# Preparing stage of a graph and attention layer: centred weights, x also loaded by features, the row norm applied where products are read

## What is computed

```python
xn = _layernorm(x, axis=-1)
h = xn @ W                                       # graph branch
deg = segment_sum(edge_weight, dst) + 1.0
dinv = rsqrt(deg)
norm = dinv[src] * edge_weight * dinv[dst]
agg = segment_sum(norm[:, None] * h[src], dst) + (dinv * dinv)[:, None] * h
k = elu(xn @ Wk.T) + 1.0                         # attention branch, 8 heads
v = xn @ Wv.T
context = einsum('bhnd,bhne->bhde', k, v)
```

## Time and profile before

| | us |
|---|---|
| median of 3 runs | 1871.64 (1870.88 to 1873.41) |
| the profiled execution, whole time | 1867.27 |
| its span in the trace | 1865.2 |
| PE busy | 1507.2 (81%) |
| POOL busy | 1020.2 (55%) |
| DVE busy | 980.8 (53%) |
| ACT busy | 521.9 (28%) |

### The profile page before, as it was taken

The page is one execution under the profiler, slowest core; times in us unless marked ns, Lnnn a source line. Parts: engine busy times, 40 slices in busy tenths (PEclk is TensorE's granted clock), DMA queues, the critical chain, the costliest instruction groups (busy, mean ns, idle before and its releaser), DMA issues. The chain is left out here.

```text
span 1865.2 us, 34354 instructions
## 1 busy us (share of the span) xinstructions
PE 1507.2 (81%) x7942; PEld 1216.4 (65%) x7943; DVE 980.8 (53%) x3382; ACT 521.9 (28%) x1456; POOL 1020.2 (55%) x1069
## 2 busy tenths in 40 slices
PE   5499986887697888698688778866479999999987
PEld 4366645665575666476576656645269989988976
DVE  8766546554446555365365517536843333343457
ACT  0144432121121121121112112101035555555533
POOL 0200016777777777777777777772035544544545
PEclk9699996999797999798799987977589999999999
DMA  6000033333333333333333333333922232354266
GB/s 224 1 0 0 0 129 98 107 105 104 101 104 104 104 104 105 101 105 105 104 103 104 104 102 104 104 105 105 178 70 96 69 118 74 93 161 144 71 206 248
DMA packets 102895, 194.20 MB, mean 104 GB/s; under 512 B 24032, under 2 KB 59360, under 8 KB 102720
## 3 DMA queue, kind: packets, MB, share of 16 engines
q0 software_dynamic: 48336, 132.17, 24.5%
q1 hardware_dynamic: 54512, 61.52, 10.9%
HBM read 160.02 MB, written 33.60 MB: 104 GB/s over the span
## 5 line engine op out<-in xcount | busy, mean ns | idle before, releaser
L707 POOL DMA_INDIRECT ring<-table,staged x784 | 747.5, 953 | 242.8 <-issue 226.9
L982 PE MATMUL bank<-ring,hots 128*128 x1372 | 324.6, 391 | 54.4 <-SPq L696 54.4
L982 PEld LDWEIGHTS bank<-ring,hots 128*128 128x128 f32 x1372 | 264.4, 195 | 104.7 <-issue 68.5
L1379 POOL DMA_INDIRECT got_x<-rows,at_x x114 | 110.2, 967 | 206.3 <-DVE at_x L1497 183.7
L982 PE MATMUL bank<-ring,late_hots 128*128 x388 | 139.9, 511 | 97.8 <-SPq L696 90.8
L1474 PEld LDWEIGHTS bank<-xT,w 128*128 128x128 f32 x1696 | 208.7, 194 | 15.5 <-issue 10.2
L1474 PE MATMUL bank<-xT,w 128*128 128x128 f32 x1696 | 209.8, 278 | 8.6 <-issue 8.6
L1447 ACT ACTIVATE hT<-bank,b 128x128 f32<-128x128 f32 x424 | 155.9, 368 | 182.7 <-PE bank L1474 158.6
L1482 PE MATMUL bank<-w,hT 128*128 128x256 f32 x848 | 201.0, 380 | 2.4 <-DVE y L1539 2.4
L792 DVE TENSOR_SCALAR hots<-iota_t,edge_l 128x128 f32<-128x128 f32 x686 | 182.4, 364 | 1.8
L982 PEld LDWEIGHTS bank<-ring,late_hots 128*128 128x128 f32 x388 | 90.9, 249 | 140.0 <-issue 126.1
(11 more groups left out here) (274 smaller groups left out, 2263.7 us busy)
## 6 DMA issues: line engine op xcount, KB each, us to landing
w<-in_w SPq DMA_DIRECT2D x32, 512.0 KB, 4.9
ring<-table,staged POOLq DMA_INDIRECT x784
got<-spread SPq DMA_DIRECT2D x11, 1024.0 KB, 8.7
x<-in_x SPq DMA_DIRECT2D x1, 6272.0 KB, 22.7
table<-xn SPq DMA_DIRECT2D x7, 896.0 KB, 4.4
rows<-xn SPq DMA_DIRECT2D x1, 6272.0 KB, 27.7
out<-out_c SPq DMA_DIRECT2D x12, 512.0 KB, 3.5
b<-in_b SPq DMA_DIRECT2D x16, 128.0 KB, 5.4
```

The costliest lines, as they stand in the source:

```text
L707: pool.indirect_dma_start(out=ring[:, j, :], out_offset=None, in_=a.table, in_offset=bass.IndirectOffsetOnAxis(ap=staged[:, half, col:col ...
L982: last = nc.tensor.matmul(agg, hot[:, k, :], two[:, k, :], start=False, stop=False)
L1379: pool.indirect_dma_start(out=got[:, n, :], out_offset=None, in_=a.rows, in_offset=bass.IndirectOffsetOnAxis(ap=at[:, n:n + 1], axis=0)).t ...
```

## The change

- **x by features.** The host also lays x out transposed (`x_cols`), and SP loads four tiles of it at a time into two slots (`xt`, 512 KB a DMA, 13 DMAs). PE multiplies it directly: no transposes and no copies of them.
- **Centred weights.** PE sums the columns of the key, graph and value weights with a matrix of ones (L474), and DVE subtracts the mean from each column (L326). A product of raw x with centred weights is the product of x minus its mean. The context sums use x times the row's rstd without its mean; the centred value weights take the mean out.
- **Norm where products are read.** ACT reads nk, pk (relu(k), new) and h with the row's rstd (or its negative) as scale. `cur` is x times rstd.
- **kk on POOL.** The sum of ek and pk is a POOL instruction (L452); DVE's L264 is gone. Four slots of `cur`, `kk` and the product bank in place of two, and the context of tile t-2 follows the keys of tile t.
- **Statistics first.** x is loaded in seven pieces, the first of seven tiles ahead of the weights. DVE starts with the statistics of these seven tiles, centres the weights, and makes batch 0; the other statistics stand between batches 1 to 5. The roots come in three parts.
- **Roots seeded on ScalarE.** ACT takes Ln and Exp as a seed, DVE refines it with one Newton step (`root`, L305). POOL's two powers are gone.
- **The tail.** The scaling of h (49 DVE instructions, L369) comes in one piece after the last root. SP issues the last piece of x_cols (tile 48) behind the first two writes of the table.
- `Combine` uses four semaphores for its loads in place of one for each; order and sizes of its DMAs stay.

```diff
-            sp.dma_start(m.x1[:], a.x.rearrange("(t p) d -> p t d", p=P)).then_inc(ld_x, 16)
-            sp.dma_start(m.weights[:], a.weights).then_inc(ld_w, 16)
-            sp.dma_start(next_i[:], a.next_cols).then_inc(ld_next, 16)
+            def columns(c):
+                if c >= 2:
+                    sp.wait_ge(kg_ok, (c - 1) * 4)
+                n = min(4, NT - c * 4)
+                sp.dma_start(xt[:, c % 2, 0:n], a.x_cols[:, c * 4:c * 4 + n]).then_inc(ld_xt[c % 2], 16)
+
+            for k, (t0, t1) in enumerate(XS):
+                sp.dma_start(m.x1[:, t0:t1], x[:, t0:t1]).then_inc(ld_x[k], 16)
+                if k == 0:
+                    sp.dma_start(m.weights[:], a.weights).then_inc(ld_w, 16)
+                if k < 2:
+                    columns(k)
+            sp.wait_ge(hot_ok, 1)
+            sp.dma_start(next_i, a.next_cols).then_inc(ld_next, 16)
...
+            for c in range(2, NT // 4):
+                columns(c)
+            stored(0)
+            stored(1)
+            columns(NT // 4)
+            for g in range(2, NT // 7):
+                stored(g)
```

DVE (`one_hots` is unchanged; `spreads` is one bn_stats a tile, `variance` the six small instructions after them):

```diff
+            def root(out, v, r, n):
+                c.add(dve.tensor_tensor(nt[:, 0:n], r, r, ALU.mult))
+                c.wait()
+                c.add(dve.scalar_tensor_tensor(nt[:, 0:n], nt[:, 0:n], -0.5, v, ALU.mult, ALU.mult))
+                c.wait()
+                c.add(dve.scalar_tensor_tensor(out, nt[:, 0:n], 1.5, r, ALU.add, ALU.mult))
+                c.wait()
...
+            spreads(0)
+            variance(0)
+            dve.wait_ge(csum_ok, 1)
+            for k, (w0, n) in enumerate(CENTRED):
+                for ch in range(DC):
+                    last = dve.scalar_tensor_tensor(m.weights[:, ch, w0:w0 + n], csum_ps[k], -1.0 / D, m.weights[:, ch, w0:w0 + n],
+                                                    ALU.mult, ALU.add)
+            last.then_inc(centred, 1)
+            one_hots(0, 0)
+            normal(0)
+            spreads(1)
+            spreads(2)
+            variance(1)
+            one_hots(1, 1)
+            normal(1)
+            one_hots(2, 0)
+            spreads(3)
+            one_hots(3, 1)
+            spreads(4)
+            one_hots(4, 0)
+            spreads(5)
+            spreads(6)
+            variance(2)
+            one_hots(5, 1)
+            normal(2)
+            with dve.Fori(0, (BATCHES - 6) // 2) as i:
                 for slot in range(2):
-                    one_hots(i * 2 + slot, slot)
...
+                    one_hots(i * 2 + (slot + 6), slot)
...
+            dve.wait_ge(seed_ok, 4)
+            root(m.dinv[:], var[:], seed[:], NT)
```

ACT, POOL and PE:

```diff
+            def keys(t, j):
+                kg, scale = kg_ps[j % 4], rstd[:, bass.ds(t, 1)]
+                if not isinstance(t, int) or t >= 4:
+                    act.wait_ge(ctx_mm, t - 2)
+                    settle(act, m)
+                act.activation(cur[:, j % 4, 0:D], tile(m.x1, t), ACT.Copy, scale=scale).then_inc(cur_ok, 1)
...
+                act.wait_ge(kg_ok, t + 1)
                 settle(act, m)
-                act.activation(nk[:], kg[:, 0:D], ACT.Relu, scale=-1.0).then_inc(nk_ok, 1)
-                act.activation(tile(hw, t), kg[:, D:2 * D], ACT.Copy).then_inc(hw_ok, 1)
+                act.activation(nk[:], kg[:, 0:D], ACT.Relu, scale=neg[:, bass.ds(t, 1)]).then_inc(nk_ok, 1)
+                act.activation(pk[:, j % 2], kg[:, 0:D], ACT.Relu, scale=scale)
+                act.activation(tile(hw, t), kg[:, D:2 * D], ACT.Copy, scale=scale).then_inc(hw_ok, 1)
                 act.wait_ge(nk_ok, t + 1)
...
+                if t == 3:
+                    seeds(1, var_ok, 2, *PARTS[1])
+                if t == 11:
+                    seeds(2, var_ok, 3, *PARTS[2])
...
+                if t == EVEN + 6:
+                    seeds(3, deg_ok, 1, 0, NT)
...
+            def keys(t, j):
+                pool.wait_ge(ek_ok, t + 1)
+                if not isinstance(t, int) or t >= 4:
+                    pool.wait_ge(ctx_mm, t - 2)
+                    settle(pool, m)
+                pool.tensor_tensor(kk[:, j % 4], ek[:, j % 2], pk[:, j % 2], ALU.add).then_inc(kk_ok, 1)
...
+            pe.wait_ge(centred, 1)
+            AFTER = {2: 1, 6: 2, 8: 3, 11: 4, 14: 5}
+            degrees(0, 0)
+            for t in range(16):
+                keys(t, t % 8, None if t % 4 else t // 8 * 16 + 16)
+                if t in AFTER:
+                    degrees(AFTER[t], AFTER[t] % 2)
+            with pe.Fori(0, 3) as i:
+                for j in range(8):
+                    keys(i * 8 + (j + 16), j, None if j % 4 else i * 16 + 48)
+                    if j % 4 != 3:
+                        n = j - j // 4
+                        degrees(i * 6 + (n + 6), n % 2)
```

More of the change, by code:

```diff
@@ L257, in one_hots @@
                 last.then_inc(hot_ok, 1)
[L259 to L268, removed]
@@ L289, in _ @@
-            dve.wait_ge(rstd_ok, 1)
-            dve.scalar_tensor_tensor(shift[:], mean[:], -1.0, rstd[:], ALU.mult, ALU.mult).then_inc(norm_ok, 1)
-            one_hots(FIRST_BATCHES + 1, 1)
-            dve.wait_ge(ld_next, 16)
-            c.add(dve.tensor_tensor(unsorted[:], dst_i[:], next_i[:], ALU.is_gt))
-            c.wait()
-            c.add(dve.reduce_sum(drops[:], unsorted[:], axis=AX.X))
[L298 to L303, removed]
@@ L336, in _ @@
             c.add(dve.tensor_scalar(m.half, m.half, 0.5, None, ALU.mult))
+            for t in range(35, NT):
+                scaled(t)
             c.wait()
@@ L355, in keys, with seeds @@
-            def keys(t, j, left=NT):
-                slot = j % 2
-                kg = kg_ps[slot]
+            act.preload_act_table_set("natural_log_exp_and_others")
+            act.sem_inc(hw_ok, 4)
+            def seeds(n, sem_in, count, t0, t1):
+                act.wait_ge(sem_in, count)
+                act.activation(ln_s[:, t0:t1], var[:, t0:t1], ACT.Ln).then_inc(ln_ok, 1)
+                act.wait_ge(ln_ok, n + 1)
+                act.activation(seed[:, t0:t1], ln_s[:, t0:t1], ACT.Exp, scale=-0.5).then_inc(seed_ok, 1)
@@ L375, in _ @@
[L375 to L386 removed]
+                settle(act, m)
+                act.activation(ek[:, j % 2], nk[:], ACT.Exp, scale=-1.0).then_inc(ek_ok, 1)
@@ L400, in _ @@
+            keys(LAST, LAST)
         @block.tensor
@@ L409, in _ @@
             pe.wait_ge(ld_const, 16)
+            pe.wait_ge(ld_w, 16)
+            for k, (w0, n) in enumerate(CENTRED):
+                for ch in range(DC):
+                    last = nc.tensor.matmul(csum_ps[k], m.ones, m.weights[:, ch, w0:w0 + n], start=(ch == 0), stop=(ch == DC - 1))
+            last.then_inc(csum_ok, 1)
             def degrees(b, slot):
@@ L450, in _ @@
-            turned(0, 0)
-            def both(i, t):
-                for half in range(2):
-                    degrees(i * 2 + FIRST_BATCHES + half, half)
-                    keys(t + 2 * half, 2 * half)
-                    keys(t + 2 * half + 1, 2 * half + 1)
-            both(0, 0)
-            with pe.Fori(1, TURNS) as i:
-                both(i, i * 4)
-            nc.tensor.matmul(deg_ps, zero[:, 0:P], zero[:, 0:3 * NT], start=False, stop=True).then_inc(deg_mm, 1)
-            for t in range(NT - LATE, NT):
-                keys(t, t % 4)
-                if t == NT - LATE + 1:
+                if not isinstance(t, int) or t >= 2:
+                    context(t - 2, (j - 2) % 8)
@@ L466, in _ @@
+            for t in range(EVEN, NT):
+                keys(t, t % 8, None if t % 4 else t // 8 * 16 + 16)
+                if t < EVEN + 4:
+                    degrees(t - EVEN + 24, (t - EVEN) % 2)
+                if t == EVEN + 3:
+                    nc.tensor.matmul(deg_ps, zero[:, 0:P], zero[:, 0:3 * NT], start=False, stop=True).then_inc(deg_mm, 1)
+                if t == EVEN + 7:
                     pe.wait_ge(deg_ok, 1)
```

218 lines of the change are left out of this document (104 added, 114 removed).

## The result

| | before | changed |
|---|---|---|
| median, four runs each | 1871.26 (1869.6 to 1873.41) | 1820.88 (1812.0 to 1823.18) |
| the profiled execution, whole time | 1867.27 | 1820.67 |
| its span | 1865.2 | 1818.8 |
| first gather of the next stage | 284.28 | 232.52 |

The changed kernel is faster: a ratio of 0.9721 (0.9687 to 0.9755). Forecast were 1821, with a range of 1812 to 1834, and a first gather near 234.

A forecast was written before the change was run, and what follows sets the result against it. Before: entry bound by DVE, then POOL; steady part by PE. Last table landing moves from 281.0 to 230.6, 50.4 less: 1867.27 becomes 1816.9, plus 4.4 for the median: 1821, range 1812 to 1834.

The forecast's parts named there:

- Entry: Start of the stage: weights land at 12.2, column sums 5.25, centring 2.5, one-hots 4.50, degrees 3.5; first keys at 28.0.
- Low clock after idling: PE in the entry runs slow after waits: column sums 5.25 (2.6 at best), degree batches 0 and 1 3.5 each.
- Batch 1: Second degree batch in the entry: PE has three tiles done at 34.2, waits 3.6 for DVE, ends the batch at 41.3.
- Seed of part 1: ACT's seed stands behind keys(3); DVE can begin batch 2 at 47.0, an added wait that holds its list for 9.
- Rate: Loop from tile 15: PE is the bound, a tile 2.63; four tiles with three batches take PE 16.3, DVE 14.9.
- DVE against POOL: POOL's kk additions beside DVE's one-hots: each costs DVE between 0 and 0.73, taken as 0.36.
- rival B: One-hots on DVE: each POOL addition costs 0.73, DVE becomes the bound; +4 to +11, 1825 to 1832; chance 0.25.
- Tail: End of the stage: scaling at 207.7, first write 209.6, DMA bounds the writes, 19.3 for 6.42 MB, last landing 230.6.
- Rival C: Table writes at the end go at the pace of another 49-tile write, 27.7 against 21.0: +6.7, 1828; chance 0.1.
- Rival D: The entry is cheaper, column sums and two batches on PE at full clock: 1813 to 1815; chance 0.15.
- Rival E: Tiles 0 to 48: PE falls to 1.2 GHz, slower than before, up to 150 more, up to 1970; chance 0.03.

The follow-up runs named there:

- number 11: The changed kernel again, without an edit, on the same chip as number 10: median 1816.18, ratio 0.9714 to the kernel before, first gather at 234.84.
- number 10: Changed kernel with the edits of number 6, number 7, Number 8, number 9, and PE's running sums two tiles earlier: median 1803.79, ratio 0.9644 to the kernel before.
- number 9: Changed kernel with 12 products of zeros on PE ahead of the column sums and 10 behind: 1812.46 in one execution, first gather at 231.56.
- Number 8: Changed kernel with degree batch 1 behind tile 4 in place of tile 2 on PE: first gather at 225.75, against 232.52.
- Number 5: Changed kernel with the seed of part 1 behind keys(0) in place of keys(3) in ACT's list: first gather at 232.70, against 232.52.
- number 1: Changed kernel with two transposes a tile put back on PE, results unused: first gather at 240.49, against 232.52.
- numbers 2: Changed kernel with every kk addition on POOL done twice, the second into an unread buffer: first gather at 240.76, against 232.52.
- number 3: Changed kernel with the 49 kk additions moved from POOL to DVE: first gather at 234.46, against 232.52.
- number 6: Changed kernel with the seed of the degrees ahead of keys(44) in place of keys(46) in ACT's list: first gather at 228.16, against 232.52.
- number 7: Changed kernel with the x_cols piece of tile 48 issued ahead of the table's writes: first gather at 232.43, against 232.52.

## Why the prediction was right, step by step

The first gather was forecast 50.4 earlier and came 51.8 earlier. The forecast of 1821 is met to 0.1, by more luck than the steps deserve: the profiled span fell by only 1865.2 - 1818.8 = 46.4. From first gather to end it is 1580.9 before and 1586.3 after, but 1581.2 in number 11, 1586.0 in number 10 and 1579.0 in number 9. The stages that nobody touched scatter by several us between executions, in part in the landing of rows: 27.7 before, and 30.4, 24.4, 25.5 and 26.2 in these four. So one whole execution tests my sum only to some 7 us, and the first gather tests it better. Two more terms cancelled: for the profiled execution the sum said 1816.9 and 1820.67 was measured, but I had added 4.4 for the median, which lay that far above the profiled execution before, and after the change it lay only 0.2 above.

- **Entry.** Weights 12.2, measured 13.19; sums 5.25, measured 5.03; centring 2.5, measured 1.95; first keys 28.0, measured 28.05. The errors cancelled: DMA a microsecond late, PE and DVE each a little faster.
- **Low clock after idling.** Right for batch 0 (3.5, measured 3.46) and batch 1 (3.5, measured 3.23). Missed: the keys behind batch 1 still took 2.40, and tile 48's 3.78, where the sum had them at full clock. The sums' 5.03 fits the low clock too, but the profile grants 1.00 from 13.2 to 18.0, so what made them slow is not shown. Number 8 shows the price of the early waits: 5.5, not the 3.4 that they last.
- **Batch 1.** PE waited 2.16 for DVE and 0.91 for POOL, forecast 3.6 for DVE alone. The term of 0.73 for a POOL addition left out its start: it stood behind hot_lo, 3.80 for two.
- **Seed of part 1.** A wait of 9 forecast, 7.58 measured, batch 2 at 46.31 (47.0). The sum said that PE would have four tiles done and wait 0.4, measured 0.30. Number 5 confirms that the wait is covered to within half a us.
- **Rate.** Four tiles and three batches 16.3; measured (177.90 - 112.93) / 4 = 16.24. PE is the bound: what number 1 gave it to do arrived at the end, and DVE's wait that number 5 removed did not.
- **DVE against POOL, rival B.** The bounds were 0 and 0.73, I took 0.36, and numbers 2 and 3 show means of 0.27 for the first addition and 0.37 for a second. In the loop DVE is busy for 73.04 / 5 = 14.6 in four tiles (forecast 14.9), 1.6 under PE. B does not hold here, but lies near: a doubled addition brought it about.
 The rows show what one meeting is: the addition starts when the DVE instruction under way has ended, and the next DVE instruction is 0.54 longer (L278, 1.40 in place of 0.86). In a round of the loop the three pairs of L282 take 2.20, 2.19 and 1.97, where number 3 has 1.66: 1.38 for four additions, 0.34 each. That some additions cost less because they fall into DVE's gaps is my reading, and was not tested. The Trainium skill, page "SBUF — State Buffer", section "Who interferes with whom", has the two exclude each other for the whole instruction. A single meeting comes near that, at 0.54 of the addition's 0.73; applied to all 49 it gave 4 to 11 us too much.
- **Tail.** Scaling 207.7, measured 206.74; first write 209.6, measured 209.16; last landing 230.6, measured about 229.4 (the last issue at 223.5 and SP's wait of 5.9). The cause was right as well: DMA is busy without a gap from 210 to 229 at 341 GB/s, where the sum had 333. The last write is issued at 223.5, when DVE's last scaling ends, but it stands behind a backlog, so DVE was not what the end waited for. Two runs bear this out: number 6 moved the first write, and the end came with it, but for the gap in DMA; number 7 changed only the order of the loads and writes, and the end stayed. Rival C would have had a last landing near 237; it did not occur. Its sign, landings of over 21 in all, was reached once: 20.2 here, but 231.8 - 210.0 = 21.8 in number 11.
- **kk on POOL** had to relieve DVE at a small price. It did not: in the loop DVE is as busy as with the additions on it (73.04 and 72.81). What number 3 lost at the end, it lost by one late addition.
- **Rival D** got nothing in the changed kernel. Numbers 8 (batch 1) and 10 (batch 0) show that the full clock is there to be had.
- **Rival E** did not occur: granted clock 1.00 between 60 and 200, with PE busy for all 140 us.
- **Not seen in advance.** The seed of the degrees in ACT's list was in the sum as a fact (199.9 to 207.7), but I did not ask what it was worth. The wait lasted 5.64, and number 6 had its first gather 4.4 earlier, 0.3 of it by an earlier start. From the degrees being ready on DVE (199.97) to their root (206.70) the changed kernel takes 6.7, not much less than POOL's power of 8.17, which the seed replaced; in number 6 it is 1.3 (199.67 to 200.96).

The balance of the 51.8: key work starts 49.7 earlier (77.79 - 28.05), and from the first keys to the first gather it is 204.5 in place of 206.5. That stretch now holds eight batches more (15.4 by the earlier trace rows); against them stand the transposes (8.0 to 13), PE's waits of 0.33 a pair, and scalings and writes that follow each other without keys between. Of these only the transposes were isolated; what centring and the scales on ACT's reads are worth by themselves was not.

Not tried: the last scalings ahead of DVE's running sums, smaller last writes, and one-hots of more than 28 columns a batch.

## What to carry to other kernels

Find the engine that sets the pace after the entry, and price each wait in the entry by what it delays there, with the slower clock that may follow added: here 3.4 us of waits cost 5.5. A seed or any other short instruction that a whole stage waits for belongs ahead of the next tile's work in its engine's list; behind it, it cost 5.4 us here, and next to nothing where the waiting engine was not the bound. Sharing work out to a second engine that reads the same memory should be priced by the time in which the first engine is busy, with and without it, and not by the lengths of instructions, which overlap: here 20 additions of 0.42 left DVE's list, and it was as busy as before. When a stage ends in a row of writes, look whether DMA has gaps before blaming the engine that feeds it.

## What the runs showed of the hardware

- **POOL beside a row of DVE scalings.** Beside L369 (float32, one tensor by a column) some additions on POOL took their usual 0.72 to 0.78 and others came to no turn until DVE's row was over. In the changed kernel the one at 222.52 took 1.55 and ended 0.59 after the row's end at 223.48; in number 7 the one at 213.66 took 3.98 and ended 0.58 after the row's end at 217.06. In number 6 two took 6.91. The clearest case is one program with two outcomes: the addition of the same tile took 0.75 at 210.54 in the changed kernel, and 6.54 at 211.37 in number 11, ending 0.58 after the row's end at 217.33. What decides between the two cases is not settled: both kinds begin in the middle of a row.
- **The low clock can begin after short waits.** Batches took 3.23 behind a wait of 2.16 (granted 0.59) and 3.52 behind 2.21 (0.52), but 2.08 behind 1.82, 2.11 behind 2.25 (number 3, granted 1.00) and 2.10 behind 0.30. PE was kept busy with zeros before the second and the third of these alike. So the length of the last wait does not decide it; what does, these readings don't show.
- **Small products beside large ones.** Two transposes delay the keys behind them by 0.21, and a tile of the loop by 0.19, though the profile shows the pair with 0.38: the lengths shown overlap.
- **Writes in a row land later**: 4.4 each before, and 4.5, 5.9 and 7.5 (least, median, most) when seven are issued in 14.3 us, with DMA at a share of 1.03 from 210 to 229.
